# A gated attention and router block on one core: the softmax weights lose a buffer, their placed copy gains one, and the written order of work is new

## The reference, cut to what matters

```
z = layernorm(x)                               # over the 2048 positions of a channel
q, k = Wq z + bq, Wk z + bk ; v = Wv ctx + bv  # 256 rows: 8 heads of 32
for each window and head:
    A = softmax(q^T k / sqrt(32) + mask)       # 128 x 128
    o = A v
x = x + tanh(g0) * (Wo gelu(o) + bo) * mask
y = layernorm(x)
w = top 8 of 64 of softmax(Wr y + rb)          # per channel row
x = x + tanh(g1) * (y * sum(w) + w @ expert_bias)
```

## Time and profile before

| what | value |
|---|---|
| median of 3 runs | 1218.3 us (1217.18 to 1219.02) |
| the profiled execution | 1222.89 us, span 1221.1 us, mean granted TensorE clock 0.988 |
| busy: PE, PEld, DVE, ACT, POOL | 93%, 86%, 80%, 84%, 58% |
| transfers of PT<-T | 1024, 80 KB each |

### The profile page before, as it was taken

One profiled execution on the slowest core, in us unless ns is written; L12 is line 12 of the kernel. 1 busy time (PEld: TensorE's weight loads), 2 busy tenths in 40 slices (PEclk: granted clock), 3 DMA queues, 4 the chain that ended last, 5 costly groups with the idle time before them and its releaser, 6 DMA issues.

```text
span 1221.1 us, 33356 instructions
## 1 busy us (share of the span) xinstructions
PE 1132.3 (93%) x11661; PEld 1046.8 (86%) x11661; DVE 982.0 (80%) x1921; ACT 1028.0 (84%) x3200; POOL 708.5 (58%) x660
## 2 busy tenths in 40 slices
PE   3799999999999999899999999999999989999976
PEld 3698999899979899788997999988998889979965
DVE  6658879988799877978789887988879877797757
ACT  4698998989988899888998889888998879988944
POOL 2376766467646676466764566646774657655621
PEclk9899999999999999999999999999999989999989
DMA  9377554885548754586546854477544874556433
GB/s 285 82 181 195 137 134 108 249 217 134 126 117 259 209 127 126 176 232 159 131 122 212 218 157 129 110 244 219 135 125 117 265 193 123 130 148 186 109 82 138
DMA packets 169767, 199.82 MB, mean 164 GB/s; under 512 B 27776, under 2 KB 104704, under 8 KB 169472
## 3 DMA queue, kind: packets, MB, share of 16 engines
q1 hardware_dynamic: 168736, 197.69, 59.4%
q10 hardware_dynamic: 864, 0.01, 0.0%
HBM read 80.06 MB, written 33.65 MB: 93 GB/s over the span
## 4 chain that ended last, share of the span: by engine, by line
PE 52%; DVE 15%; SPq 15%; issue 7%; POOL 4%; ACT 4%; DMA 3%; DVEq 0%; POOLq 0%; ACTq 0%
SPq L520 10%; PE ring L309 7%; PE ring L311 6%; PE ring L310 6%; PE ring L365 4%; DVE X L894 3%; PE ring L348 3%; PE ring L324 3%; PE ring L326 3%; PE ring L325 3%; PE ring L384 3%; PE ring L385 3%; PE ring L386 3%; PE ring L403 3%; SPq L525 2%
## 5 line engine op out<-in xcount | busy, mean ns | idle before, releaser
L614 ACT ACTIVATE P<-ring,nmx 128x128 f32<-128x128 f32 x1024 | 358.7, 402 | 55.5 <-DVE nmx L755 55.1
L309 PE MATMUL ring<-z_hi,wqk_hi 128*128 128x256 f32 x1024 | 298.6, 292 | 23.5 <-DVE z_lo L958 21.1
L311 PE MATMUL ring<-z_lo,wqk_hi 128*128 128x256 f32 x1024 | 291.4, 285 | 0.0
L310 PE MATMUL ring<-z_hi,wqk_lo 128*128 128x256 f32 x1024 | 291.3, 285 | 0.0
L614 ACT ACTIVATION_READ_ACCUMULATOR P<-ring,nmx 128x1 f32 x1024 | 248.5, 243 | 0.0
L1049 POOL TENSOR_TENSOR z_lo<-z,z_hi 128x1024 fp32r<-128x1024 f32 x62 | 147.6, 2380 | 164.5 <-ACT z_hi L582 164.5
L309 PEld LDWEIGHTS ring<-z_hi,wqk_hi 128*128 128x128 f32 x1024 | 197.3, 193 | 36.3 <-DVE wqk_lo L933 21.1
L1061 POOL TENSOR_TENSOR X<-X,xt 128x512 f32<-128x512 f32 x128 | 165.2, 1290 | 100.9 <-DVE xt L790 100.5
L762 DVE STREAM_TRANSPOSE T<-P 128x512 f32<-128x512 f32 x256 | 169.1, 690 | 42.5 <-ACT P L614 24.4
L311 PEld LDWEIGHTS ring<-z_lo,wqk_hi 128*128 128x128 f32 x1024 | 197.8, 193 | 0.0
L310 PEld LDWEIGHTS ring<-z_hi,wqk_lo 128*128 128x128 f32 x1024 | 197.7, 193 | 0.0
(11 more groups left out here) (138 smaller groups left out, 2713.3 us busy)
## 6 DMA issues: line engine op xcount, KB each, us to landing
PT<-T SPq DMA_DIRECT2D x1024, 80.0 KB, 2.1
cx<-in_ctx SPq DMA_DIRECT2D x128, 256.0 KB, 3.7
out_y<-X SPq DMA_DIRECT2D x128, 256.0 KB, 3.1
X<-in_x SPq DMA_DIRECT2D x112, 256.0 KB, 4.2
mg<-in_mask SPq DMA_DIRECT2D x64, 128.0 KB, 3.1
X<-in_x SPq DMA_DIRECT2D x8, 512.0 KB, 7.6
sel<-rows_d SPq DMA_DIRECT2D x256, 3.0 KB
X<-in_eb SPq DMA_DIRECT2D x2, 512.0 KB, 8.5
```

The lines of the kernel that those rows point to most:

```text
L309: e.matmul(o, wqk_hi[:, t, cols], z_hi[:, t, :], t == 0, False)
L310: e.matmul(o, wqk_lo[:, t, cols], z_hi[:, t, :], False, False)
L311: last = e.matmul(o, wqk_hi[:, t, cols], z_lo[:, t, :], False, t == DT - 1)
L614: last = e.activation(P[:, n, :], bank("S", 4 * u + g)[:, k * W:(k + 1) * W], ACT.Exp, bias=nmx[u % 2][:, n:n + 1], accum_out=den[u % 2][: ...
```

## The change: what it does

- `P` is gone. ACT writes exp straight into `T[u % 2]`, in four runs of 32 elements, and DVE turns the blocks in place. `expo(u)` now waits for `move(u - 2)` to have landed instead of for the turning of unit u - 1.
- `PT` has two buffers with a semaphore each. `move(u)` waits for `divide(u - 2)`.
- The weights of the router, `w2`, lie in `L`; `c_logits` waits for two steps of the batch before as well.
- `SLOTS` and `ENDS` have new numbers, so the order on every engine is another. Modulo 16, before and after: on TensorE WO second half 1 and 0.5; q 2 and 4.5; v 5.25 and 4.75, 10 and 8.75; hT 5.5, 5.75 and 5.75, 7.25; PV 9.25 and 6; k 9.75 and 6.75; WO first half 11.25 and 10.75; S 14.25 and 14; R 15.25, 15.5 and 14.75, 0.25. On SP rows 2 and 0.5, mask 2 and 9.25, context 2.25, 7 and 2, 6, `move` 8.5 and 6. On DVE `top` 1 and 0, `turn_d` 7.25 and 5.75, `divide` 7.25 and 6.25, second xt 3.5 and 1.75. On ACT exp 4 and 1.5.

```diff
@@ SLOTS (ENDS, the shifts of the last three units, has new numbers too)
-    rows=-30, z32=-26.25, z_hi=-16, z_lo=-19.75, q=-14, q_ev=-6.25, k=-6.25, k_ev=-6.25,
-    c_hi=-15.5, c_lo=-13.75, v=-10.75, v_ev=-7.5, v_gap=-3.25,
-    S=-1.75, top=1, exp=4, e_gap=0.25, tp=6.25, td=7.25, mv=8.5, PV=25.25, on=23.25,
-    gelu=23, mg=2, ot_hi=24, ot_lo=27.5, WO=27.25, WO_gap=5.75, xt=29.75, x1=31, bn2=39.25,
-    hT=37.5, hT_gap=0.25, ht_hi=41.25, ht_lo=41.75, R=47.25,
-    norm2=27.5, c_base=33.5, L=36, LT=34, c_top=38.75, c_exp=37.75, c_w=40.75, c_sc=40.75, wT=43, wt_hi=43.25, wt_lo=42.25, mix=43.75, m_gap=0.25,
-    sx=44.75, sx_gap=1.25, x2=45.25, rl=48.5, rl_gap=2,
-    x_1=21, x_gap=3.5, bn1=63.25, bn1_gap=2, norm1=101.25,
+    rows=-31.5, z32=-26.75, z_hi=-16, z_lo=-21.5, q=-11.5, q_ev=-4.75, k=-9.25, k_ev=-6.75,
+    c_hi=-16, c_lo=-14, v=-11.25, v_ev=-8.75, v_gap=-4,
+    S=-2, top=0, exp=1.5, e_gap=0.25, tp=5.25, td=5.75, mv=6, PV=22, on=22.25,
+    gelu=20.75, mg=9.25, ot_hi=21.25, ot_lo=25.75, WO=26.75, WO_gap=5.75, xt=28, x1=28.25, bn2=39.25,
+    hT=37.75, hT_gap=1.5, ht_hi=39.75, ht_lo=41.5, R=46.75,
+    norm2=27, c_base=34.75, L=34.5, LT=37, c_top=38, c_exp=36, c_w=38.5, c_sc=41, wT=39.5, wt_hi=42, wt_lo=42, mix=44.5, m_gap=0.25,
+    sx=42.25, sx_gap=1.25, x2=44.25, rl=47.5, rl_gap=2,
+    x_1=9.75, x_gap=4, bn1=62.25, bn1_gap=2.25, norm1=100.25,
@@ buffers
-        P = sb("P", [128, 16, W])
-        PT = sb("PT", [128, 4, 20, 32])
+        PT = [sb(f"PT{i}", [128, 4, 20, 32]) for i in range(2)]
-        w2 = sb("w2", [128, DT, 2, NX])
+        w2 = L[:].rearrange("p (t a x) -> p t a x", t=DT, a=2)
-        pt_in = sem("pt")
+        pt_in = [sem(f"pt{i}") for i in range(2)]
@@ weigh (PT -> PT[u % 2] in its matmuls and in divide)
-                e.wait_ge(pt_in, 256 * (u + 1))
+                e.wait_ge(pt_in[u % 2], 256 * (u // 2 + 1))
@@ move
-                if u:
-                    e.wait_ge(on_v, u)
+                if u >= 2:
+                    e.wait_ge(on_v, u - 1)
-                        e.dma_start(PT[32 * b:32 * b + 32, a, :, :], T[u % 2][32 * a:32 * a + 32, b, :, :]).then_inc(pt_in, 16)
+                        e.dma_start(PT[u % 2][32 * b:32 * b + 32, a, :, :], T[u % 2][32 * a:32 * a + 32, b, :, :]).then_inc(pt_in[u % 2], 16)
@@ expo
-                if u:
-                    e.wait_ge(tp_v, 4 * (u - 1) + g + 1)
+                if u >= 2:
+                    e.wait_ge(pt_in[u % 2], 256 * (u // 2))
-                    last = e.activation(P[:, n, :], bank("S", 4 * u + g)[:, k * W:(k + 1) * W], ACT.Exp,
-                                        bias=nmx[u % 2][:, n:n + 1], accum_out=den[u % 2][:, n:n + 1])
+                    last = e.activation(T[u % 2][:, :, n, :], bank("S", 4 * u + g)[:, k * W:(k + 1) * W].rearrange("p (b j) -> p b j", b=4),
+                                        ACT.Exp, bias=nmx[u % 2][:, n:n + 1], accum_out=den[u % 2][:, n:n + 1])
@@ c_logits
                     e.wait_ge(lt_pe, b)
+                    e.wait_ge(wT_pe, b)
+                    e.wait_ge(ac_v, b)
@@ turn_p (turn_d: its wait becomes pt_in[u % 2], 256 * (u // 2))
-                if u >= 2:
-                    e.wait_ge(pt_in, 256 * (u - 1))
                 e.wait_ge(exp_a, 4 * u + g + 1)
-                e.transpose(T[u % 2][:, :, 4 * g:4 * g + 4, :].rearrange("p b k i -> p k b i"),
-                            P[:, 4 * g:4 * g + 4, :].rearrange("p k (b j) -> p k b j", b=4)).then_inc(tp_v, 1)
+                tg = T[u % 2][:, :, 4 * g:4 * g + 4, :].rearrange("p b k i -> p k b i")
+                e.transpose(tg, tg).then_inc(tp_v, 1)
```

More of the change, by code:

```diff
@@ L364, in weigh @@
                             o = bank("PV", u)[32 * g:32 * g + 32, m * U + w * W:m * U + (w + 1) * W]
-                            last = e.matmul(o, v32[p % NV][:, h * DH:(h + 1) * DH], PT[:, :, 4 * g + 2 * m + w, :], True, True)
+                            last = e.matmul(o, v32[p % NV][:, h * DH:(h + 1) * DH], PT[u % 2][:, :, 4 * g + 2 * m + w, :], True, True)
                 last.then_inc(pv_pe, 1)
@@ L778, in divide @@
                                 bank("PV", u)[:].rearrange("p (k a i) -> p k a i", k=4, a=4),
-                                PT[:, :, 16:20, :].rearrange("p a k i -> p k a i"), ALU.mult).then_inc(on_v, 1)
+                                PT[u % 2][:, :, 16:20, :].rearrange("p a k i -> p k a i"), ALU.mult).then_inc(on_v, 1)
             def weigh_out(u, j):
@@ L865, in c_weights @@
                 e.wait_ge(wm_v, 4 * b + 2)
-                e.tensor_tensor(w2[:], ex[:].unsqueeze(2).to_broadcast([128, DT, 2, NX]),
+                e.tensor_tensor(w2, ex[:].unsqueeze(2).to_broadcast([128, DT, 2, NX]),
                                 sc[:, :, 3:4].unsqueeze(3).to_broadcast([128, DT, 2, NX]), ALU.mult).then_inc(w2_v, 1)
```

## The result

The changed kernel takes 1230.45 us (median of 4, 1229.78 to 1231.8) against 1217.74 (4 runs, 1210.26 to 1219.02): ratio 1.0096, interval 1.0065 to 1.0127. It is slower by 12.7 us, about 1%, where I forecast 12.1 us less. The profiled execution takes 1229.78 us (span 1228.0), that of before 1222.89 (span 1221.1).

A forecast was written before the change was run, and what follows sets the result against it. TensorE was taken as the bound, so only removed stops of it count. Terms -9 - 4 + 0 - 0.6 + 1.5 = -12.1 took the profiled 1222.9 us to 1210.8, a median of 1206; forecast range 1197 to 1214, overall 1193 to 1228.

The forecast's parts named there:

- Exp, turning in place, L: Exp into T and turning in place cost at most 10 ns each, under the slack; L's added waits are met: 0.
- Ordinary units: Units without x loads or mixing stay at 15.92 us: 0, with +1.5 us charged for the spread of the context landing.
- Load units: The three units per batch that load x: excess 4.2 us instead of 5.7, times six batches: -9.
- The relief before hT: One piece of statistics instead of two before the second xt, hT half a slot later: TensorE's stops before hT shrink.
- the wait of 1.86 for x: VectorE's statistics in the load units: this wait goes with later slots, the one of 3.58 us stays or grows.
- Mix units: Units with router and mix: TensorE stops of 2.1 us for 2.7, seven times: -4.
- `w_turn`'s term: TensorE's stop before turning the router's placed weights in a mix unit: 0.6 us where the rows show 0.3.
- Start: Head of the kernel: exp ahead of two weight copies, cx_hi about 1 us later, first moves sooner: 0, with 2 either way.
- End: Chain after the last scores: the last moves no longer wait for divide: -0.6 us.
- Rival A: The context behind the moves lands late and WO stops: up to +26 us, about +10 for half, 1228; chance 0.26.
- B: Rival: issuing the moves does not delay what stands behind them, the stops at WO don't come: 1190 us; chance 0.13.
- The comparison that I made there: Against the rival of 1190 us: moves take 10.7 to 11.9 us of SP's time, issuing five times the 2.1 us landing.

The follow-up runs named there:

- e1: The changed code with SLOTS and ENDS of the kernel before: 1216.11 us, ratio 0.9972 to the kernel before.
- e3: The changed kernel with the second context load put ahead of the moves on SP again: 1227.54 us, ratio 1.0082 to the kernel before.
- e7: The changed kernel with the 96 loads of x from batch 2 on issued by GpSimd instead of SP: 1214.68 us, ratio 0.9972 to the kernel before.
- e10: The changed kernel with the steps of the last three units that ENDS names on their old ticks: 1231.39 us, ratio 1.0107 to the kernel before.
- e8: The changed code in the order of before, with the 96 loads of x issued by GpSimd: 1239.60 us, ratio 1.0166 to the kernel before.

## Why the prediction was wrong

- **Exp, turning in place, L: 0.** Right: e1's ratio is 0.9972, and 405 and 682 ns stand against 402 and 690.
- **Ordinary units: 0, with 1.5 for the context.** Right: 15.92 becomes 15.93. Moves start 0.6 us after the turn's end (598.57 after 597.95) where I had 0.3. The context is late 26 times, at most 3.1 us, and e3 gives 2 to 3 us for it, which is not clear of zero.
- **Load units: -9.** This step failed first, and by its base. I took 5.7 us from the one batch of the earlier trace rows. Over the six batches of the same trace the excess was 2.3, 3.1, 5.7, 4.1, 3.0 and 7.2 us, 4.2 in the mean, which is exactly what I forecast for after. It came to 4.4, so that forecast was met and the saving still was none. In the batch that I had read it fell from 5.7 to 3.9, though in other units than I had drawn (16.6, 19.2 and 15.9 us for 17.9, 17.6 and 16.5). The relief before hT was real (12.6 us to none), and it went to the next wait: 11.1 us before the scores. I had written that the wait of 1.86 for x would go and that of 3.58 stay or grow. In that batch the first went and the second grew to 4.71; in all six the sum went from 29.4 to 33.5, with a second wait of 2.2 to 3.1 us in three batches. What I did not draw: the queue behind the moves was the bound, and nothing in the change took a transfer out of it. VectorE reached the piece 10.5 us after the scores (547.78 less 537.31) instead of 12.2, and the data came at 15.2 instead of 15.7. e7 shows it from the other side.
- **Mix units: -4.** Wrong in sign: +3.0. I had stops of 0.6 us for w_turn, 0.8 for WO and 0 for the mix; they are 2.5, 0.3 and 0. What failed is `w_turn`'s term, 0.6 for 2.5. My walk along exp, L, c_top, c_exp and c_weights did not name the router's base, nearly 4 us ahead of the turning, two operations of which last 1.3 us each. But the base stood ahead of the turning before as well (3.2 us, now 3.9), so that it explains at most 0.7 of the 2.3 us by which the stop grew; the larger part is that TensorE comes 1.3 us earlier. And I priced no clock for a stop of this length: it is 0.86 over 12 us in five of the seven. That these stops make up the +3.0 is argued; no run took them away.
- **Start: 0 within 2.** Held (+0.8; +2.2 against e1). **End: -0.6.** The part that I priced is there: the last moves start 9.6 us after the scores (1175.45 less 1165.85), 10.3 before. What I left out are the new numbers in `ENDS`: the division, xt and what follows in the last units come 1 to 3 us later, +2.65 in all, of which e10 gets 1.5 back in its trace and nothing in its median.
- **Rival A** had the time about right (1228) with the wrong mechanism: ordinary units did not stretch, and e3 refutes it. **B** is refuted: the context and the loads of x behind the moves are late, as the issue takes 10.6 us. The comparison that I made there is of 16 issues with one landing; one issue is 0.6 to 0.7 us against 2.1, so what the trace contradicts is that the issuing of 16 in a row can be left out. The sum of my terms and the measured one differ by 19.0 us: 10.0 in the load units, 7.0 in the mix units, 3.2 at the end, 0.8 in the head, less 2.0 in the ordinary units.
- From profile to median 5.8 us more are lost (12.7 for 6.9). That is 5.2 by which the profiled execution of before lies over its median and 0.7 by which the other lies under its own. Where these 5.8 us fall stands in no trace.

What stays open: how much of the loss is clock, why the new order leaves the DMA engines room that the old one does not, and whether one move of four blocks at a time would free SyncE's queue by itself, which wasn't tried.

## What to carry to other kernels

A saving per batch must be based on all batches of the trace: the one batch that was looked at closest was 1.5 us over the mean, which times six is the whole gain that I forecast for these units. When a queue is full, relief elsewhere only brings the next consumer sooner to the same wait; ask what leaves the queue, and take that out first (here the x loads, 16 us). But a full queue also spaces its transfers out, and the same step can overfill the DMA engines and stop another consumer (here 23 us the other way). Before a run with moved numbers is read, look whether the order on any engine changed, and whether the step that others wait for moved with the rest: of two such experiments here one changed nothing and one left the last turning where it was.

## What the runs showed of the hardware

- Two VectorE operations of 128x4 take 0.16 and 0.22 us where GpSimd is idle (end of the trace), and 1.28 and 1.33 beside it. They end when a GpSimd operation ends (497.73 and 498.98):

```profile
495.18 1.29 POOL L1060 TENSOR_TENSOR X<-X,xt 128x512 f32<-128x512 f32 x1
496.44 1.29 POOL L1054 TENSOR_TENSOR cx_lo<-cx,cx_hi 128x512 fp32r<-128x512 f32 x1
497.69 1.29 POOL L1060 TENSOR_TENSOR X<-X,xt 128x512 f32<-128x512 f32 x1
```

```profile
1205.42 0.16 DVE L827 TENSOR_TENSOR dm<-ln 128x4 f32<-128x4 f32 x1 [1.20 <-POOL ln L1069]
1205.50 0.22 DVE L828 TENSOR_SCALAR gate<-ln,cst 128x4 f32<-128x4 f32 x1
```

The Trainium skill, SBUF — State Buffer, section Who interferes with whom, says that VectorE and GpSimd share a pair of ports as an exclusive lock and that the later one blocks fully, for operations with two SBUF inputs among others. The trace agrees in these rows, but not in every one: the next operation with two inputs (L830, at 499.03) took 0.19 us though a GpSimd operation had begun at 498.96; in the other six units it took 0.49 and ended with GpSimd's.
- GpSimd issues a 256 KB load in 0.56 us, and such a load lands in 4.5 us (e7), as SyncE's do (4.7).
- The stops of 2.2 to 2.6 us before `w_turn` are followed by a granted clock of 0.86 over 12 us in five of the seven units of the changed kernel and in two of the seven of e7; in the others it stays at 1.00. A stop of 2.6 us in e8, with little work ahead of it (1.49 of 4 us busy), is followed by 0.57 over 8 us.
